# A vision tower on one core: where the random features are scaled, and when expert 2's first weights are loaded

## The reference

```python
h = tok(x)                                  # patches times a weight
h = h + attn0(layernorm(h))                 # softmax attention, 16 heads
h = h + moe0(layernorm(h))                  # 8 experts, top 2 per token
h = h + attn1(layernorm(h))                 # random features, 16 heads
h = h + moe1(layernorm(h))                  # 8 experts, top 2 per token

# moe0, expert e, for the tokens that chose it:
hid = silu(x @ w1[e]) * (x @ w3[e])         # 256 -> 1024
out = (hid @ w2[e]) * gate                  # 1024 -> 256

# attn1, per head:
proj = q @ rf.T                             # 64 random features
phi  = concat([cos(proj), sin(proj)]) * exp(-|q|^2 / 2) / 8
```

## Time and profile before

| | before |
|---|---|
| median of 3 executions | 351.67 us (351.13 to 352.06) |
| the profiled execution, its own time | 353.31 us |
| span of the profiled execution | 351.2 us |
| mean granted TensorE clock | 0.986 |
| TensorE busy | 319.8 us (91%) |
| GpSimd busy | 227.1 us (65%) |
| VectorE busy | 220.9 us (63%) |
| ScalarE busy | 173.3 us (49%) |
| bytes moved by DMA | 64.57 MB, mean 184 GB/s |

### The profile page before, as it was taken

The page is one execution under the profiler, slowest core; times in us unless marked ns, Lnnn a source line. Parts: engine busy times, 40 slices in busy tenths (PEclk is TensorE's granted clock), DMA queues, the critical chain, the costliest instruction groups (busy, mean ns, idle before and its releaser), DMA issues.

```text
span 351.2 us, 9645 instructions
## 1 busy us (share of the span) xinstructions
PE 319.8 (91%) x3715; PEld 271.6 (77%) x3730; DVE 220.9 (63%) x690; ACT 173.3 (49%) x454; POOL 227.1 (65%) x168
## 2 busy tenths in 40 slices
PE   7998899998898999998989999999999899999980
PEld 4886687876668999998965876878887588898860
DVE  2646457586476566666558818577977835556656
ACT  1155455554134454544443358777761546655650
POOL 0489975858459999999984006703417447597873
PEclk9999999999899999999999999999999999999996
DMA  7999950004004999999213920000000259999624
GB/s 255 385 402 410 398 215 3 30 2 152 2 31 141 366 354 392 375 385 347 92 37 94 384 90 2 0 2 0 32 4 30 74 177 321 302 311 329 231 80 119
DMA packets 28245, 64.57 MB, mean 184 GB/s; under 512 B 3440, under 2 KB 9008, under 8 KB 25904
## 3 DMA queue, kind: packets, MB, share of 16 engines
q1 hardware_dynamic: 26672, 59.89, 47.9%
q0 software_dynamic: 1536, 4.20, 3.9%
HBM read 54.70 MB, written 9.37 MB: 182 GB/s over the span
## 4 chain that ended last, share of the span: by engine, by line
PE 60%; DVE 13%; DMA 8%; POOL 7%; issue 5%; ACT 4%; SPq 2%; POOLq 0%; DVEq 0%
PE ps L1049 8%; PE ps L1051 7%; PE ps L1050 7%; PE ps L1544 4%; DMA xe<-slots_dram 4%; PE ps L1769 4%; PE ps L1556 4%; PE ps L1530 3%; POOL area_y L815 2%; PE ps L1103 2%; DMA slots_dram<-ye 1%; DVE hot L428 1%; PE ps L563 1%; PE ps L610 1%; PE ps L564 1%
## 5 line engine op out<-in xcount | busy, mean ns | idle before, releaser
L1049 PE MATMUL ps<-xeT,wslot 128*128 128x0 bf16 (+1 forms) x384 | 69.3, 222 | 6.1 <-DVE hid L1161 2.4
L1050 PE MATMUL ps<-xeT,wslot 128*128 128x0 bf16 (+1 forms) x384 | 69.0, 221 | 0.0
L1306 POOL TENSOR_TENSOR area_w<-wslot 128x2048 bf16<-128x2048 f32 (+2 forms) x18 | 51.0, 2843 | 10.2 <-DMA wslot<-blob_dram 10.2
L1293 POOL TENSOR_TENSOR area_q<-wslot 128x2048 bf16<-128x2048 f32 x16 | 57.4, 3604 | 0.4 <-DMA wslot<-blob_dram 0.4
L1293 POOL TENSOR_TENSOR area_w<-wslot 128x1024 bf16<-128x1024 f32 x16 | 30.0, 1893 | 31.6 <-DVE area_q L1449 23.5
L1161 DVE TENSOR_TENSOR hid<-ps,hid 128x160 bf16<-128x160 f32 x112 | 35.2, 320 | 23.3 <-ACT hid L1118 22.3
L1051 PE MATMUL ps<-xeT,area_q 128*128 128x0 bf16 (+1 forms) x256 | 45.5, 221 | 0.0
L1049 PEld LDWEIGHTS ps<-xeT,wslot 128*128 128x128 bf16 x384 | 37.5, 98 | 8.8 <-DVE hid L1161 4.2
L1049 PE MATMUL ps<-hid,wslot 128*128 128x0 bf16 (+1 forms) x224 | 40.0, 221 | 0.8 <-POOL area_w L1306 0.7
L1050 PE MATMUL ps<-hid,wslot 128*128 128x0 bf16 (+1 forms) x224 | 39.9, 221 | 0.0
L1051 PE MATMUL ps<-hid,area_w 128*128 128x0 bf16 (+1 forms) x224 | 39.9, 221 | 0.0
(11 more groups left out here) (240 smaller groups left out, 924.7 us busy)
## 6 DMA issues: line engine op xcount, KB each, us to landing
wslot<-blob_dram SPq DMA_DIRECT2D x32, 1024.0 KB, 7.6
wslot<-blob_dram SPq DMA_DIRECT2D x16, 512.0 KB, 6.4
slots_dram<-hid SPq DMA_DIRECT2D x8, 544.0 KB, 10.6
xe<-slots_dram SPq DMA_DIRECT2D x14, 128.0 KB, 4.7
slots_dram<-ye SPq DMA_DIRECT2D x14, 128.0 KB, 5.1
area_x<-x_dram SPq DMA_DIRECT2D x4, 384.0 KB, 6.5
area_w<-wq_dram SPq DMA_DIRECT2D x2, 512.0 KB, 8.9
area_w<-wk_dram SPq DMA_DIRECT2D x2, 512.0 KB, 9.5
```

The costliest lines, as they stand in the source:

```text
L1049: nc.tensor.matmul(out, w_high[:, s, high_at:high_at + P], x_high, start=first, stop=False)
L1050: nc.tensor.matmul(out, w_high[:, s, high_at:high_at + P], x_low, start=False, stop=False)
L1293: nc.gpsimd.tensor_tensor(half_of(w_low1[L][:, s, :], L, half), half_of(wslot[:, s, :], L, half), half_of(w_high[:, s, :], L, half), ALU.s ...
L1306: ins = nc.gpsimd.tensor_tensor(w_low2[:, s, part], wslot[:, s, both], w_high[:, s, both], ALU.subtract)
```

## The change

Two edits. In layer 0, SyncE waits for the first four blocks of expert 0 and issues the first half of expert 2's first-layer weights before it waits for the scatters and loads the rows of expert 1. The rest of its list keeps its order. And the scaling of the random features leaves GpSimd's queue, where it stood between the low parts of expert 1 and those of expert 2, and becomes a ScalarE activation with a scale, at the head of layer 1's projections.

```diff
--- before.py
+++ after.py
@@ -1340,13 +1340,20 @@
                 sp.dma_start(rows_of(e, 0, P), ye[:, s, 0, :]).then_inc(m.stored[s], 16)
                 sp.dma_start(rows_of(e, P, CT), ye[0:CT, s, 1, :]).then_inc(m.stored[s], 16)
 
+            def load_next(e, half):
+                sp.wait_ge(m.gu_full, KF * e + HF * (half + 1))
+                load_first(sp, L, blob, e + 2, e % 2, half)
+
+            if L == 0:
+
+                load_next(0, 0)
             sp.wait_ge(scattered, 16 * 2 * NT * (L + 1))
             load_rows(sp, m, 1, 1)
             for e in range(E):
                 if e + 2 < E:
                     for half in range(2):
-                        sp.wait_ge(m.gu_full, KF * e + HF * (half + 1))
-                        load_first(sp, L, blob, e + 2, e % 2, half)
+                        if (L, e, half) != (0, 0, 0):
+                            load_next(e, half)
                     load_rows(sp, m, e + 2, e % 2)
                     sp.wait_ge(m.y_full, KD * (e + 1))
                     load_second(sp, L, blob, e + 2, e % 2)
@@ -1417,6 +1424,8 @@
             norms(NT - 1)
 
         def project1_act(act):
+            act.wait_ge(small_ld, 96)
+            nc.scalar.mul(rfs[:], rfb[:], 1.0 / TWO_PI).then_inc(rfs_ready, 1)
             act.wait_ge(ln_done[2], 1)
             nc.scalar.activation(early[:, 0:1], const[:, C_ONE:C_ONE + 1], ACT.Exp)
             for t in range(NT):
@@ -1721,8 +1730,6 @@
                 scatter(pool, 0, t, xn)
             for s in range(2):
                 low_second(pool, 0, s, s)
-            pool.wait_ge(small_ld, 96)
-            nc.gpsimd.tensor_scalar(rfs[:], rfb[:], 1.0 / TWO_PI, None, ALU.mult).then_inc(rfs_ready, 1)
             moe_pool(pool, 0)
             for t in range(NT):
                 gather(pool, 0, t)
```

## The result

| | changed | before, same job | ratio, 95% interval |
|---|---|---|---|
| first measurement, 4 executions each | 357.36 us (355.8 to 360.56) | 351.87 us (351.13 to 353.38) | 1.0164 [1.0115, 1.0212] |
| second, 12 executions (35 before) | 354.25 us | 353.17 us | 1.0043 [1.0004, 1.0082] |
| third, 12 executions (33 before) | 354.26 us | 352.44 us | 1.0042 [1.0014, 1.0070] |

The ratios leave out executions that took over 1.5% longer than the fastest of their kernel; the medians in microseconds are of all of them.

The account below looks back on a forecast made before the run. GpSimd's chain in layer 0's expert stage was taken to set the end. 115.38 + 1.5 (d) + 1.5 (r) + 5.2 = 123.58 against 122.92, +0.66 us: 351.67 + 0.66 = 352.3 us, range 350.1 to 353.1.

Parts of the forecast that it names:

- chain: GpSimd's products in layer 0's expert stage, to its last for expert 7: forecast to end 0.66 us later.
- d: Before expert 1's row turn in layer 0, TensorE waits longer for rows behind the early load: 1.5 us (0.85 to 2.15).
- r: TensorE's loss at 1.2 GHz at the start of expert 0's second layer: 1.5 us (1.0 to 1.7).
- release of the slot, before: TensorE ends expert 0's second layer and expert 2's second-layer weights are issued: 115.38 in the trace before.
- second-layer weights, from issue to GpSimd's product: Load of expert 2's second-layer weights, which GpSimd waits for: 5.2 us rather than 7.0.
- the rows pass the load: Rival, chance 0.18: expert 1's rows overtake the early load, d below 0.6, clock holds; 349.8 to 350.0 us.
- Whether the clock falls: Before expert 1's row turn, TensorE's idle time grows to about 2.4 us; clock expected to fall in most executions.
- They find a less crowded queue: Loads behind expert 2's second-layer weights are issued later by d but meet a less crowded queue; no cost was added.
- the second-layer weights come late: Rival, chance 0.15: GpSimd waits longer for expert 2's second-layer weights, landing at 124.73; +1.8 us, 353.5 us.
- the clock holds: Rival, chance 0.24: TensorE keeps its clock through the row-turn wait, r = 0; -0.84 us, 350.8 us.

Follow-up runs that it names:

- after: The changed kernel's profiled execution in the first measurement, slowest of its four: 360.56 us; that measurement's ratio to the kernel before was 1.0164.
- again: The unaltered changed kernel measured a second time, against the kernel before: 354.25 us, ratio 1.0043.
- again2: The unaltered changed kernel measured a third time, paired with a version whose wait was filled with products: 354.26 us, ratio 1.0042 to the kernel before.
- 1.5 MB ahead: Changed kernel plus another 0.5 MB load, into an area nobody reads, ahead of expert 1's rows: 356.76 us, ratio 1.0088 to the kernel before.
- 0.5 MB much earlier: Against the version with 0.5 MB ahead, that piece is issued after two blocks of expert 0 instead of four: 355.21 us, ratio 1.0052 to the kernel before.

## Why the prediction was wrong

**What held.** The half load was forecast for 107.38 and issued at 107.72 and 107.30. The first GpSimd product for expert 2 was forecast for 113.93 and came at 114.36 and 113.97. The order of waits was as written down: rows late, row turn late, second-layer weights late, GpSimd waits for them. TensorE, released up to 5.1 us late, still had to wait for GpSimd's last product at the end of the stage, 0.68 us in the first profile (0.74 before), so the chain set the end. ScalarE's part cost nothing.

**What failed is the size of the terms**, first of all that of d, the 1.5 us that the rows were to come later: it was 2.50, 2.26, 2.27 and 2.08 us in the four profiles with 1 MB ahead and the turn in its place ("after", "again", the half load alone, "again2"), beyond its upper bound in three of them. The loss r was forecast as one size of 1.5 us; it was 0 twice and 2.64 and 2.89 us, 1.4 on average. And a wait that was put at nothing came in at 0.35 to 0.43 us. The table is in the time of the trace of before; the chain starts 0.44 us later in the first profile and 0.05 later in the second (the one of "again"), which is taken off.

| term | forecast | first profile | second profile |
|---|---|---|---|
| release of the slot, before | 115.38 | 115.38 | 115.38 |
| d, rows behind the early load | 1.5 (0.85 to 2.15) | 2.50 | 2.26 |
| r, loss at 1.2 GHz | 1.5 (1.0 to 1.7) | 2.64 | 0 |
| second-layer weights, from issue to GpSimd's product | 5.2 | 4.99 | 5.03 |
| GpSimd's product starts (122.92 before) | 123.58, +0.66 | 125.51, +2.59 | 122.67, -0.25 |
| expert 3's first half | none | +0.42 | +0.42 |
| chain | +0.66 | +3.05 | +0.20 |

(The last line is measured. Its sum from the two lines above it leaves 0.04 us in the first profile and 0.03 in the second.)

- *d.* I took 5.2 us for the half load's landing, between 4.9 and 5.5. It took 6.0 and 5.7 us. And I took the middle between 0 and 0.7 us behind it for the rows. The last row piece landed at 114.34, 0.6 us behind the half at 113.72, nearly the whole 0.7. Both choices were too small and add up to nearly 1 us. With 1 MB ahead and the turn in its place TensorE waited 3.0 to 3.4 us in every profile: the rival in which the rows pass the load (d below 0.6) is refuted. The Trainium skill ("DMA: Bandwidth & Descriptors", on queues, rings and completion order) says that each DMA engine takes its descriptors in ring order, that a later one may finish its write before an earlier one, and that the semaphore increment lands only behind every earlier write of that engine. So it doesn't say that small rows get past a whole load, and the trace agrees, by the 0.6 us that the rows landed behind it.
- *r.* The slow stretch of the earlier trace rows lasted 3.4 us. Behind this wait it lasted 6.84, 6.84 and 6.82 us ("after", "again2", 1.5 MB ahead), twice as long, and most of it lay on work: 2.64, 2.89 and 2.40 us lost, where I had bounded it by 1.7. With 0.5 MB ahead it lasted 3.40 us at the same place and cost 1.65 us, inside the forecast's bounds. One stretch was taken for the length of all of them; the profiles have two lengths, and what makes the longer one isn't shown.
- *Whether the clock falls.* I argued from the length of the idle time, 1.4 us borne and 1.73 not. The runs refute that as a measure: it fell behind 1.96, 3.00, 3.42 and 4.69 us and held behind 3.19 and 3.21. The idle time of 1.73 us at 88 that the forecast rested on is in all fourteen profiles with the same length, and in two of them (the half load alone, and 0.5 MB much earlier) the clock held behind it: a look at one profile couldn't show that. With 1 MB ahead, nothing filled in and the turn in its place, it fell in 2 of 4 profiles. The Trainium skill ("TensorE: Matmul & The Clock Gate", part 1) says that the number of slow matmuls at a kernel's start changes from run to run of one kernel. The profiles here show the like in the middle of one: 3.21 us borne and 3.00 us not, in the same kernel. Four profiles are too few to hold against the forecast's chances.
- *The loads behind it.* "They find a less crowded queue" was costed at nothing. Expert 3's first half is issued 3.1 us behind the delayed load and landed 5.8 us later, and GpSimd waited 0.42 us for it in the first two profiles and 0.35 in "again2"; before, that product followed without a gap. With the clock held, this term turns -0.25 into +0.20. It isn't the early load's alone: in the kernel before, this half landed at 126.4, hardly 0.1 us before it was wanted at 126.48, and with the ScalarE part alone GpSimd waited 0.36 us for it.

Where the clock held, the chain's +0.20 us lies within the forecast's own range, and that is luck: against the forecast's sum the 1.5 us of r weren't lost, and 0.8 us more of d and 0.4 us of the neglected wait took most of that back.

The two outcomes also give the size. The four profiles with 1 MB ahead have chains 3.05 and 2.80 us (fallen) and 0.20 and 0.23 us (held) longer than before, 1.57 us on average. The longer measurements' ratios of 1.0042 and 1.0043 are 1.5 us too. That a share of executions near one half loses the clock is inferred from these, not counted in the timed ones, which have no profile.

Of the rivals, "the second-layer weights come late" with its 0.15 is what happened when the clock fell, through its own mechanism but beyond its +1.8 us; "the clock holds" is the other outcome, worth +0.2 and not -0.84, by the larger d and the neglected wait.

**The first profile's other 3.9 us** are in the rest, and one place there shows itself, at the row turn of the expert stage of layer 1. TensorE's timeline and clock:

```profile
327.41 0.33 PE L883 MATMUL ps<-const,xe 128*128 128x128 f32 x1 [2.60 <-DMA xe<-slots_dram]
```

```profile
327.00:328.00 1.00, 0.59 (x5) 1.00 1.03 362
328.00:329.00 1.00, 1.00 (x9) 0.58 1.05 398
...
331.00:332.00 1.00, 1.00 (x11) 0.71 0.07 28
```

A row piece took 7.9 us to land and the clock fell for 3.4 us. In the kernel before this turn stands at 321.40 without an idle time, so of the 3.91 us 2.52 have come up by 327.41 (with the 3.49 that lie ahead taken off). The diff touches nothing of layer 1's loads, and in all other profiles of this study the rest is 170.5 to 173.0 us. That speaks for chance, as do the later medians of 354.3 us where the first four executions took 355.8 and more; but the cause isn't shown and stays open.

## What to carry to other kernels

A large load moved ahead in a queue is paid by whatever small load stood behind it: find who waits for that small one, and which buffer this waiter releases, before counting the gain. Here the gain came in full on the chain (-1.9 us; 1.8 and 0.9 us by the medians of the times) once the waiting step was put behind work that was ready. And a wait added to TensorE is priced twice, with the clock held and with it fallen, and the second price is half of the work that the slow stretch covers: here 1.65 us for a stretch of 3.4 and 2.4 to 2.9 us for one of 6.8. One profile shows one of the outcomes only; profile the same kernel again before its clock goes into a sum.

## What was not expected of the hardware

- The clock's fall isn't decided by the length of one wait: the same kernel held 2.4 GHz through 3.21 us of idle time and lost it in 3.00 us. An idle time of 1.73 us, the same in all fourteen profiles, lost it in twelve and not in two. When it fell at the row turn, the low level lasted 6.8 us in three profiles, although TensorE worked without a gap from the turn on, and 3.4 us in one; at 88 us and 328 us it lasted 3.4.
- With a load of 0.5 MB issued beside the scatters' writes, they ended 3.92 us after the last was issued, against 2.41 to 2.44 without (one profile).
- Each 0.5 MB ahead of rows of 16 KB and 128 KB in the same queue delayed them by 1.3 us on average (from 0.7 to 0.9 us of wait up to 4.69).
